# GpSimd normalises the value blocks of an image in place of scaled weights and a bias row; some query activations move one slot later

## The reference, cut to what matters

```
x = x + L0(gn(x))     # y * sigmoid(gate): a gate per channel, from the pooled channels and three sampled taps
x = x + L1(gn(x))     # local attention

def _gn(v, G=32, eps=1e-05): ...   (g - m) / sqrt(s + eps), over 4 channels and all pixels

L1: value = v_w y + v_b
    keyf, query = relu(bn(W2 relu(bn(W1 y))))
    sim over the 27 neighbours of a pixel (3 x 3, dilations 1, 2 and 4), softmax
    context = sum(sim * value of neighbour);  out = w_w context + w_b
```

## Time and profile before

| what | value |
|---|---|
| median of 3 runs | 1502.79 us (1501.54 to 1503.92) |
| the profiled execution's own time | 1504.14 us |
| its span, first to last instruction | 1502.4 us, granted TensorE clock 0.998 |
| TensorE matmul busy | 1452.5 us, 97% |
| TensorE weight load busy | 1189.1 us, 79% |
| VectorE busy | 1240.1 us, 83% |
| ScalarE busy | 1163.9 us, 77% |
| GpSimd busy | 824.5 us, 55% |

### The profile page before, as it was taken

One profiled execution on the slowest core, in us unless ns is written; L12 is line 12 of the kernel. 1 busy time (PEld: TensorE's weight loads), 2 busy tenths in 40 slices (PEclk: granted clock), 3 DMA queues, 4 the chain that ended last, 5 costly groups with the idle time before them and its releaser, 6 DMA issues.

```text
span 1502.4 us, 35364 instructions
## 1 busy us (share of the span) xinstructions
PE 1452.5 (97%) x9159; PEld 1189.1 (79%) x9159; DVE 1240.1 (83%) x4631; ACT 1163.9 (77%) x3044; POOL 824.5 (55%) x2313
## 2 busy tenths in 40 slices
PE   1799999999999999999999999999999999999998
PEld 0588888888888888888888888888888888888886
DVE  6488888888888888888888888888888888888876
ACT  2487787887787887787887787887787887787876
POOL 5645565654565654565655565654565655565620
PEclk9999999999999999999999999999999999999999
DMA  2244544454543454544454543454544455543344
GB/s 92 77 123 149 166 111 119 145 166 149 165 116 115 145 166 149 165 106 125 145 166 149 167 115 115 144 166 150 166 107 124 144 166 150 163 123 112 101 122 142
DMA packets 104708, 205.97 MB, mean 137 GB/s; under 512 B 13632, under 2 KB 83776, under 8 KB 96448
## 3 DMA queue, kind: packets, MB, share of 16 engines
q1 hardware_dynamic: 103632, 203.49, 45.8%
q10 hardware_dynamic: 880, 0.23, 0.1%
HBM read 51.62 MB, written 51.38 MB: 69 GB/s over the span
## 4 chain that ended last, share of the span: by engine, by line
PE 94%; POOL 2%; issue 2%; DVE 1%; ACT 1%; ACTq 0%; POOLq 0%; DVEq 0%
PE ps_s L432 23%; PE ps_o L465 20%; PE ps_v L505 12%; PE ps_t L444 11%; PE ps_p L487 11%; PE ps_p L482 11%; PE ps_o L470 3%; PE ps_v L521 1%; PE ps_v L533 1%; PE ps_v L525 1%; POOL hats L767 0%; PE ps_v L528 0%; ACTq L585 0%; POOL xb L836 0%; PE ps_v L532 0%
## 5 line engine op out<-in xcount | busy, mean ns | idle before, releaser
L597 ACT ACTIVATE e<-e,zmin 128x256 f32<-128x256 f32 x800 | 402.8, 503 | 125.0 <-DVE zmin L969 120.4
L969 DVE CUSTOM_DVE_ANT_0 e<-ps_s,mask 128x256 f32<-128x256 f32 x800 | 338.3, 423 | 175.4 <-PE ps_s L432 166.3
L465 PEld LDWEIGHTS ps_o<-eT,v 128*128 128x128 f32 x2688 | 380.3, 191 | 85.3 <-issue 81.6
L465 PE MATMUL ps_o<-eT,v 128*128 128x128 f32 x2688 | 433.4, 276 | 0.1
L432 PE MATMUL ps_s<-kk,qq 128*128 128x256 f32 x1408 | 425.2, 384 | 0.1
L444 PE MATMUL ps_t<-ident,e 128*128 128x128 f32 x1600 | 305.7, 273 | 0.0
L612 ACT ACTIVATE eT<-ps_t 128x512 f32<-128x512 f32 (+1 forms) x416 | 235.7, 567 | 78.2 <-PE ps_t L444 75.8
L444 PEld LDWEIGHTS ps_t<-ident,e 128*128 128x128 f32 x1600 | 225.2, 141 | 80.5 <-issue 0.2
L432 PEld LDWEIGHTS ps_s<-kk,qq 128*128 128x128 f32 x1408 | 223.6, 192 | 47.7 <-issue 41.2
L986 DVE SCALAR_TENSOR_TENSOR e<-e,rz,keep 128x256 f32<-128x256 f32 x480 | 246.0, 513 | 17.1
L505 PE MATMUL ps_v<-wvox,xb 128*128 128x128 f32 x1600 | 219.9, 278 | 0.9 <-DVE v L1007 0.8
(11 more groups left out here) (150 smaller groups left out, 1809.8 us busy)
## 6 DMA issues: line engine op xcount, KB each, us to landing
out_dram<-raw SPq DMA_DIRECT2D x32, 1568.0 KB, 5.7
raw<-in_x_dram SPq DMA_DIRECT2D x31, 1568.0 KB, 6.6
v<-v SPq DMA_DIRECT2D x192, 224.0 KB, 2.9
kk<-kk SPq DMA_DIRECT2D x192, 112.0 KB, 2.2
ksp<-kk SPq DMA_DIRECT2D x192, 64.0 KB, 2.1
v<-v_last SPq DMA_DIRECT2D x64, 128.0 KB, 2.9
kk<-kk SPq DMA_DIRECT2D x32, 224.0 KB, 2.9
v<-v_last SPq DMA_DIRECT2D x64, 96.0 KB, 2.7
```

The source lines that it names most:

```text
L465: last = nc.tensor.matmul(o[:, UPIX * (u - 1):UPIX * (u + 1)], v[:, s, u, :], eT[:, UPIX * (base + 2 * u - 1):UPIX * (base + 2 * u + 1)], ...
L597: nc.scalar.activation(e[:, i, :], e[:, i, :], ACT.Exp, bias=zmin[:, i:i + 1], scale=-1.0, accum_out=zs[:, i:i + 1]).then_inc(e_done.next( ...
L969: nc.vector.tensor_tensor_reduce(e[:, i, :], ps_s[(TILES * n.parity() + t) % 2][:, 0:KEYS], mask[:].rearrange("p s h a b -> p (s h a b)"), ...
```

## The change

GpSimd's `spread` writes `x * Y_A + Y_B` into `xb` in place of a copy, so block by block a `tensor_scalar` with two per-channel operands takes the place of a `tensor_copy`. The values' matmul then uses the unscaled weights `wvoT`, made once, and VectorE adds `wobv`, also made once. The scaled weights `wvox`, the row `yb_row`, the second matmul of `c6` (L533) and the `bias` step of `d13` (L1066) go; block 0 waits for step 31 of the chain (`pg`).

The chain's GpSimd steps become 32 for an image in place of 40: the correction of the inverse root takes four steps in place of five, `diag` is made with two operands, a step ROOT = VE * R is added in `p3`, the VectorE steps of the gate give `RG` directly, `p7` has six steps in place of ten (four in place of seven up to `of_x1`'s variance), and `pw` has one in place of three. `p11` now waits for `c6` of two images before, and `c6` waits for `w1x` (31) in place of `yb_row` (38).

The queries of strips 0, 2, 3 and 6 run two slots behind their hidden matmul in place of one, after that slot's copy and exponential.

```diff
+QUERIES_LATER = (0, 2, 3, 6)
-CHAIN_READS = ((2, "d1"), (4, "d4"), (13, "d9"), (16, "d13"))
-N_DG, N_PG, N_CG, N_AG = 16, 40, 4, 4
+CHAIN_READS = ((2, "d1"), (4, "d4"), (13, "d9"), (15, "d13"))
+N_DG, N_PG, N_CG, N_AG = 15, 32, 4, 4
...
                             last = nc.tensor.matmul(ps_v[:, P * j:P * (j + 1)], pixels,
-                                                    wvox[:, m.parity(), :], start=True, stop=True)
+                                                    wvoT[:], start=True, stop=True)
...
                         if at == CH["c6"]:
-                            pe.wait_ge(pg.sem, pg.count(m, 38))
-                            nc.tensor.matmul(ps_v[:, 0:1], w1T[:], col(Y_B + m.parity()), start=True, stop=True)
-                            nc.tensor.matmul(ps_v[:, P:2 * P], yb_row[:], wvoT[:], start=True,
+                            pe.wait_ge(pg.sem, pg.count(m, 31))
+                            nc.tensor.matmul(ps_v[:, 0:1], w1T[:], col(Y_B + m.parity()), start=True,
                                              stop=True).then_inc(cg.next(), 1)
...
                                 if rel == at + 1:
                                     keys(m, g)
+                                if rel == at + (2 if g in QUERIES_LATER else 1):
                                     queries(m, g)
...
-                                    lambda: gp.tensor_tensor(t, to, to, ALU.mult),
-                                    lambda: gp.tensor_tensor(t, t, ve, ALU.mult),
+                                    lambda: gp.tensor_scalar(t, to, to, ve, ALU.mult, ALU.mult),
...
-                                  lambda: gp.tensor_tensor(col(PL), col(D), col(R), ALU.mult),
-                                  lambda: gp.tensor_scalar(diag[:], ident[:], col(PL), None, ALU.mult))
+                                  lambda: gp.tensor_scalar(diag[:], ident[:], col(D), col(R), ALU.mult, ALU.mult),
+                                  lambda: gp.tensor_tensor(col(ROOT), col(VE), col(R), ALU.mult))
...
-                            steps(18,
-                                  lambda: gp.tensor_tensor(col(RG), col(R), col(GATE), ALU.mult),
-                                  lambda: gp.tensor_tensor(col(T0), col(RG), col(D), ALU.mult),
-                                  lambda: gp.tensor_tensor(moment(of_x1, MEAN), col(T0), moment(of_x, MEAN), ALU.add),
+                            steps(17,
+                                  lambda: gp.tensor_scalar(moment(of_x1, MEAN), col(D), col(RG), moment(of_x, MEAN),
+                                                           ALU.mult, ALU.add),
                                   lambda: gp.tensor_scalar(moment(of_x1, APART, GN), spread_s[:], moment(of_x1, MEAN),
                                                            None, ALU.mult),
                                   lambda: gp.tensor_scalar(a, col(RG), 1.0, None, ALU.add),
-                                  lambda: gp.tensor_tensor(col(T0), a, a, ALU.mult),
-                                  lambda: gp.tensor_tensor(moment(of_x1, VAR), col(T0), moment(of_x, VAR), ALU.mult),
-                                  lambda: gp.tensor_tensor(col(M1G), moment(of_x, MEAN), col(D), ALU.subtract),
-                                  lambda: gp.tensor_tensor(col(M1G), col(M1G), col(RG), ALU.mult),
+                                  lambda: gp.tensor_scalar(moment(of_x1, VAR), moment(of_x, VAR), a, a, ALU.mult,
+                                                           ALU.mult),
+                                  lambda: gp.tensor_tensor(col(M1G), moment(in_x, MEAN), col(RG), ALU.mult),
...
-                            steps(28, variance(col(VE1), col(SQ1), in_x1), *rsqrt(col(R1), col(VE1), col(T0)),
+                            gp.wait_ge(cg.sem, cg.count(m + -2, 4))
+                            steps(23, variance(col(VE1), col(SQ1), in_x1), *rsqrt(col(R1), col(VE1), col(T0)),
...
-                            gp.wait_ge(v_ps.sem, v_ps.count(m + -2, COLUMNS))
-                            gp.wait_ge(cg.sem, cg.count(m + -1, 4))
-                            steps(37,
-                                  lambda: gp.tensor_scalar(yb_row[:], ones[:], col(Y_B + i), None, ALU.mult),
-                                  lambda: gp.tensor_scalar(w1x[:, i, :], w1T[:], col(Y_A + i), None, ALU.mult),
-                                  lambda: gp.tensor_scalar(wvox[:, i, :], wvoT[:], col(Y_A + i), None, ALU.mult))
+                            steps(31, lambda: gp.tensor_scalar(w1x[:, i, :], w1T[:], col(Y_A + i), None, ALU.mult))
...
                         if b == 0:
+                            gp.wait_ge(pg.sem, pg.count(m, 31))
...
-                            gp.tensor_copy(to[:, 0, 0:HALO, cs], rows[:, H - HALO:H, at])
-                            gp.tensor_copy(to[:, 0, HALO:SIDE, cs], rows[:, 0:HALO, at])
-                            last = gp.tensor_copy(to[:, 1:CHUNKS, :, cs], rows[:, HALO:H - HALO, at].rearrange(
-                                "p (n r) c -> p n r c", r=SIDE))
+                            for k, rs, src in ((0, slice(0, HALO), rows[:, H - HALO:H, at]),
+                                               (0, slice(HALO, SIDE), rows[:, 0:HALO, at]),
+                                               (slice(1, CHUNKS), slice(0, SIDE), rows[:, HALO:H - HALO, at].rearrange(
+                                                   "p (n r) c -> p n r c", r=SIDE))):
+                                last = gp.tensor_scalar(to[:, k, rs, cs], src, col(Y_A + m.parity()),
+                                                        col(Y_B + m.parity()), ALU.mult, ALU.add)
...
-                                                bias[:, m.parity(), :].unsqueeze(1).to_broadcast([P, last - first, P]),
+                                                wobv[:].unsqueeze(1).to_broadcast([P, last - first, P]),
...
-                            step(11, nc.vector.tensor_scalar(col(EX), col(EX), 1.0, None, ALU.add))
-                            step(12, nc.vector.reciprocal(col(GATE), col(EX)))
+                            dve.wait_ge(pg.sem, pg.count(m, 9))
+                            step(11, nc.vector.scalar_tensor_tensor(col(EX), col(EX), 1.0, col(ROOT), ALU.add, ALU.mult))
+                            step(12, nc.vector.reciprocal(col(RG), col(EX)))
...
-                            step(16, nc.vector.tensor_tensor(bias[:, m.parity(), :], ps_v[:, P:2 * P], wobv[:],
-                                                             ALU.add))
```

More of the change, by code:

```diff
@@ L213, in build @@
         w1x = sb("w1x", [P, 2, P])
-        wvox = sb("wvox", [P, 2, P])
         b1x = sb("b1x", [P, 2])
-        yb_row = sb("yb_row", [P, P])
-        bias = sb("bias", [P, 2, P])
         hid = sb("hid", [P, SPIX])
@@ L324, in chain_at @@
                     yield m, rel
-        D, SQ, VE, R, T0, PL, POS, ZS, EX, GATE, RG, SQ1, VE1, R1, BM, M1G = (
-            0, 1, 2, 3, 4, 5, 6, 9, 10, 11, 12, 15, 16, 17, 18, 20)
+        D, SQ, VE, R, T0, ROOT, POS, ZS, EX, RG, SQ1, VE1, R1, BM, M1G = (
+            0, 1, 2, 3, 4, 5, 6, 9, 10, 12, 15, 16, 17, 18, 20)
         MEAN, VAR, APART = 0, 1, 2
@@ L478, in hidden @@
                             pe.wait_ge(dg.sem, dg.count(m, 15))
-                            pe.wait_ge(pg.sem, pg.count(m, 40))
+                            pe.wait_ge(pg.sem, pg.count(m, 32))
                         pe.wait_ge(q_done.sem, q_done.count(m, g))
@@ L523, in chain @@
                         if at == CH["c3"]:
-                            pe.wait_ge(pg.sem, pg.count(m, 10))
+                            pe.wait_ge(pg.sem, pg.count(m, 8))
                             nc.tensor.matmul(ps_v[:, 8:8 + P], ones[:], diag[:], start=True, stop=True).then_inc(cg.next(), 1)
                         if at == CH["c4"]:
-                            pe.wait_ge(pg.sem, pg.count(m, 25))
+                            pe.wait_ge(pg.sem, pg.count(m, 21))
                             nc.tensor.matmul(ps_v[:, 0:2 + GN], group_avg[:], of_x1[:], start=True,
@@ L662, in slot @@
                                 act.wait_ge(dg.sem, dg.count(m, 9))
-                                act.wait_ge(pg.sem, pg.count((m + -1), 16))
+                                act.wait_ge(pg.sem, pg.count((m + -1), 15))
                                 for k in range(TAPS):
@@ L767, in tap @@
                                         lambda: gp.tensor_scalar(hat, hat, 0.0, wg_s[:, 9 + k:10 + k], ALU.max, ALU.mult))
-                            steps(10, *tap(0), *tap(1), *tap(2),
+                            steps(9, *tap(0), *tap(1), *tap(2),
                                   lambda: gp.tensor_tensor(hat_sum[:], hats[:, 0, 1, :], hats[:, 1, 1, :], ALU.add),
@@ L1047, in chain @@
                         if at == CH["d6"]:
-                            dve.wait_ge(pg.sem, pg.count(m, 18))
+                            dve.wait_ge(pg.sem, pg.count(m, 17))
                             step(10, nc.vector.scalar_tensor_tensor(junk[:], pooled_row[:], 1.0, hat_sum[:],
```

## The result

| what | before | after |
|---|---|---|
| median of 9 runs each | 1501.84 us (1500.86 to 1503.92) | 1505.82 us (1504.64 to 1508.3) |
| ratio, 95% interval | | 1.0023 (1.0014 to 1.0032) |
| span of the profiled execution | 1502.4 us | 1506.6 us |

The changed kernel is slower by 0.23%, 4.0 us, where 1489 us was forecast, 13.9 us less than before. The first scores come 1.4 us earlier (56.0 us instead of 57.4), the first image takes 1.9 us longer (49.55 instead of 47.62 us from its first scores to those of the second), and every further image takes 45.12 us instead of 45.01 (medians over the images between, from score matmul to score matmul).

A forecast was written before the change was run, and what follows sets the result against it. TensorE was taken as the bound, at 45.0 us an image. The terms -6.9 - 9.0 - 3.1 + 0.6 + 5.4 - 0.9 = -13.9 us took the median of 1502.79 to 1489 us, range 1482 to 1498.

The forecast's parts named there:

- the signs that it had named for being wrong: An image still taking over 44.85 us, or TensorE waiting for the queries of group 6 or for blocks.
- bias matmul L533: On TensorE, removing this matmul saves net 0.22 us an image, 6.9 us over 31 images.
- wait at `c1`: At L521, removing VectorE's bias step ends TensorE's wait: 0.30 us an image, 9.0 us over 30 images.
- `eT` copy, slot 0: At slot 0, group 2's later queries let ScalarE's copy start sooner: 0.10 us an image, 3.1 us saved.
- wait at `c4`: At L528, slower GpSimd blocks delay `of_x1`: 0.18 us an image lost, 5.4 us; bounds 0 and 0.48 us an image.
- queries of strip 6 before L480: At the hidden matmul, later queries leave 0.13 us; cost 0.02 us an image, 0.6 us, bounds 0 to 0.3 an image.
- the price of a block: On GpSimd, a value block by tensor_scalar takes 1.13 to 1.34 us, middle 1.23, instead of 0.75.
- Rival (c): Waits come back at `c4` at its upper bound or at group 0's hidden matmul: 1498 us; chance 0.24.
- Rival (d): TensorE is not the bound, or the waits eat all the gain: 1500 to 1505 us; chance 0.06.
- Rival (b): No wait at `c4`, with blocks at the low bound or `p7` faster than taken: 1483.5 us; chance 0.20.
- Rival (e): GpSimd blocks run at 2.7 ns an element, about 1.9 us each, TensorE losing at `c4`: about 1528 us; chance 0.03.
- The rule of 2.6 cycles for an element: On GpSimd at 1.2 GHz, a block would take 1.7 us and the kernel about 1517 us; chance 0.03.

The follow-up runs named there:

- early blocks: The changed kernel with value blocks 4 and 5 five slots earlier on GpSimd: 1494.57 us, 0.9939 of the kernel before.
- copies: The changed kernel with plain copies in the value blocks, their normalisation left out: 1504.82 us, 1.001 of the kernel before.
- the copied kernel: The changed kernel with plain copies in the value blocks and the shifts of strips 1 and 2 later on GpSimd: 1504.69 us, 1.0012 of the kernel before.

## Why the prediction was wrong

The mechanisms of the sum are all in the trace, and three of them had their size. The forecast failed on the two terms for new waits, and the signs that it had named for being wrong all came: 45.12 us an image against its 44.85, and waits for blocks and for the queries of strip 6. Per image of the steady part, in us:

| term of the sum | forecast | measured | by |
|---|---|---|---|
| bias matmul L533 | -0.22 | -0.22 | start distances |
| wait at `c1` | -0.30 | -0.31 | gap 0.22 + own passes 0.09 |
| `eT` copy, slot 0 | -0.10 | -0.10 | gap 0.10, gone |
| wait at `c4` | +0.18 | +0.62 | gap 0.52 + own passes 0.10 |
| queries of strip 6 before L480 | +0.02 | +0.25 | gap 0.18 + own passes 0.07 |
| values in slot 4 (-0.07) and smaller ones | 0 | about -0.13 | start distances |
| sum | -0.42 | +0.11 | period 45.12 - 45.01 = +0.11 |

The change was +4.0 us for -13.9, so it was missed by 17.9 us; the time itself by 16.8, since the median before went from 1502.79 in three runs to 1501.84 in nine. 0.53 us in each of 30 images is 15.9 us of it. The head with the first image is another 1.4: -1.4 + 1.9 = +0.5 us instead of -0.9. The last image and terms counted for 31 images make up the rest.

The -0.07 of slot 4 hangs on the `c4` wait: the eight value passes took 0.97 us before (L505) and take 0.90 behind a late `c4`, and 0.97 again in every run without that wait. So the wait costs about 0.54 us net, and the spread passes at L505 were a sign, in the trace before, that this place had nothing to spare.

**Bias matmul and `c1` wait: right.** The run without them took 0.53 us off an image. Here the list of waits said next to nothing, and the start distances of the earlier trace rows said all of it. The Trainium skill, "Perfetto Trace Analysis", section "Identifying the Most-Contended Engine", would have weight loads (and the share of peak FLOP/s) tell the headroom. Here the trace disagrees: the loads were busy for 36.92 of 45.00 us, and yet taking 0.52 us from the matmul queue gave 0.53.

**`c4`: the named mechanism, mis-sized.** The step that failed is the price of a block: 1.23 us taken (bounds 1.13 to 1.34), 1.55 measured. From the start of block 4 to that of `p7` an image took 2.00 us before (0.25 of it spare) and 3.10 after: 1.10 more and not 0.71. `p7` gave what was taken (0.55 saved for 0.53), so `of_x1` came 0.56 us later instead of 0.18, and the blocks started 0.05 later against TensorE; less 0.09 of room that is the 0.52 measured.

The block of 0.75 us before was off too, the other way. The first of the two copied blocks took 1.00 us (602.39 to 603.39), for its first small copy was already stretched to twice its length:

```profile
602.39 0.40 POOL L834 COPY xb<-raw 128x32 f32<-128x32 f32 x1
```

It ran beside VectorE's L986 at 602.18, below. So the row that spoke against pricing a block from a quiet place was in the trace before. The two errors partly cancelled: with 0.75 us for both copied blocks, blocks of 1.55 would have cost 0.25 us more than they did. The six pieces of the two blocks in the changed kernel, by the tile's view of that stretch (shortest, median and longest ns):

```profile
L830 POOL TENSOR_SCALAR xb<-raw,g x6: 363/584/657, 603.9 to 606.4; 128x32 f32<-128x32 f32 x4, 128x384 f32<-128x384 f32 x2
```

Undisturbed, a block is 0.34 + 0.34 + 0.64 = 1.33 us from start to start, the upper bound; the lower one had its small piece (0.27) from a step with a single per-channel operand, and the form with two has a higher floor. The first small piece of each block, though, took 0.64 and 0.53 us instead of 0.36 in this stretch, beside VectorE, which adds 0.22 a block. No bound had that: the price came from L812, one long step in a quiet place. VectorE's timeline there shows the other side of it:

```profile
603.50 0.68 DVE L980 SCALAR_TENSOR_TENSOR e<-e,rz,keep 128x256 f32<-128x256 f32 x1
...
604.97 0.82 DVE L980 SCALAR_TENSOR_TENSOR e<-e,rz,keep 128x256 f32<-128x256 f32 x1
```

The same two steps of the kernel before:

```profile
602.18 0.54 DVE L986 SCALAR_TENSOR_TENSOR e<-e,rz,keep 128x256 f32<-128x256 f32 x1
...
603.56 0.48 DVE L986 SCALAR_TENSOR_TENSOR e<-e,rz,keep 128x256 f32<-128x256 f32 x1
```

**Strip 6's queries: the named mechanism, mis-sized.** I had 0.13 us left and called it about enough. Two numbers were off. A release of L480 by ScalarE takes 629.16 - 628.90 = 0.26 us, not the 0.14 read at L521: the price of a hand-over was carried from one matmul to another that has a further wait instruction behind the late one (why it takes longer was not tested). And the masking step was to come 0.42 us earlier with the bias step gone; it ends at 627.35 for queries that end at 628.90, with an aggregate only about 0.33 us earlier against TensorE, so 0.08 of the 0.13 us were left. 0.26 - 0.08 is the gap of 0.18. The 0.07 that a waiting matmul then spends in its own passes had been priced at `c4` and was left out here.

**The rivals.** Rival (c) named both places, and they came at once, where each had been priced as if alone: 1498 for one of them, and 1489 + 13.2 + 6.9 = 1509 for both as measured, 1505 with the -0.13 us of the small terms. At `c4` even its upper bound, 0.48, was passed. Rival (d) has the nearest time: of its two cases "the waits eat all" came true, and that TensorE is not the bound is refuted by the run without the bias matmul. Rival (b) fell with the wait at `c4`. Rival (e) put its turning point at a block over 1.45 us and 0.64 us of loss at `c4`; 1.55 and 0.62 were measured, and the time fell near the line of no change. That is luck in part: by its own sum 1.55 gives 0.82, and the 1.00 us of the copied block brings it down. Its reason was another too (the form's floor and the overlap, and not 2.7 ns an element).

The rule of 2.6 cycles for an element (the Trainium skill, "GPSIMD Engine Reference", section 3.1) does not describe these steps: 384 elements took 0.66 us, and an element beyond the 32 of a small piece (0.64 - 0.34) / 352 = 0.85 ns. The section gives the figure for tensor_tensor, which reads two tensors; the prediction carried it to a step that reads one.

**What no part of the sum had** is VectorE. With the `c4` wait taken away (early blocks or copies), `in_x` at L503 was the next in line with 0.3 to 0.6 us, so at most a part of what `c4` costs could be won back there. I had asked what is late next only on the queue in which the wait stands.

## What to carry to other kernels

Price a step from a row with the same neighbours on the other engine, not from the quietest one, and price a row of short steps by the row. Where elementwise steps of two engines run side by side, ask which of the two the critical engine waits for: moving a step so that the other engine pays can be worth more than making it cheaper. When several new waits have little room each, their cases aren't alternatives; add them up.

## What the runs showed of the hardware

- Some VectorE and GpSimd elementwise steps stretch each other. A scaling step of 128 x 256 with two tensors takes 0.485 us alone (all 141 that met nothing of GpSimd in the kernel before took 0.483 to 0.489) and 0.54 to 0.82 in the rows above, beside a GpSimd tensor_scalar or copy; a TENSOR_SCALAR with one tensor (L977) 0.35 and 0.76; a one-element gate step 0.15 and 0.45; a GpSimd piece of 32 elements 0.36 and 0.53 to 0.64.
- Not every overlap does it: VectorE's masking (0.42 us), the final addition and the statistics (0.62 each), which read PSUM or a single tensor, kept their length within 0.03 us in all their overlaps, in the kernel before and in the changed one.
- The Trainium skill, "GPSIMD Engine Reference", section 8 "Key points", says that GpSimd shares its SBUF interfaces with VectorE, in contention with VectorE instructions that have two SBUF inputs or run in a 2-port mode. The rows of the scaling and gate steps agree; that L977 ran in such a mode no trace shows. Two such stretches cost TensorE 0.66 us an image in the copied kernel.
- Mostly the step that started later was the stretched one: in the kernel before a small copy took 0.40 us (median of 60) when it started behind a two-tensor scaling step and 0.21 (median of 31) when it started ahead of one. Where both started within some 0.1 us it was VectorE's in one kernel and GpSimd's in another. What decides there stays open.
- A matmul that waited spreads its own passes: 0.24 instead of 0.14 us at `c4`, 0.07 us more at L480 and at L503 (there with a gap of 0.02 already).
- From the end of the releasing step to the matmul's start it is 0.15 us at L526 and 0.26 at L480. In its queue L480 has another wait instruction behind the one that is late; that this is the reason was argued from the order of instructions, and not tested.
- A small tensor_scalar on GpSimd with two per-channel operands takes 0.34 us for one element and 0.36 for 32, with one such operand 0.26 to 0.31 (1 to 4 elements), with constants alone 0.19 to 0.23, and a tensor_tensor 0.19 (0.57 with a power, L735). From start to start two tensor_tensor of the chain take 0.54 us, and the step that stands for both 0.43 (607.43 - 607.00): merging them saves 0.1 us.
